# A four-stage transformer block on one core: another order of the steps in the opening and the first feed-forward

## The reference

```python
x = x + tanh(gx[0]) * wkv(time_decay, time_first, k=layernorm(x), v=ctx)      # time mix: a scan over tokens
x = x + tanh(gf[0]) * (mlp(layernorm(x)) + peer(layernorm(x)))                # feed-forward 1024 wide, and look-up experts
x = x + tanh(gx[1]) * gated_linear_attention(layernorm(x), ctx)               # 16 heads, keys and values from ctx
x = x + tanh(gf[1]) * (top-2 of 8 experts + shared expert)(layernorm(x))

# peer: queries -> two sets of 64 scores -> top 8 of each -> top 8 of the 64 sums -> 8 of 512 rows,
#       silu(x . down_row) * softmax(score), times up_row, summed
# attention: kv_summary = sum over tokens of feature(k) (x) v,  feature(k) = k + 1 if k > 0 else exp(k)
```

## Time and profile before

| | |
|---|---|
| runs | 507.08, 507.49, 510.03 us |
| the profiled execution | 508.22 us, span 506.4 us |
| TensorE busy | 450.3 us, 89% |
| its weight loads | 356.1 us, 70% |
| VectorE | 347.2 us, 69% |
| ScalarE | 247.2 us, 49% |
| GpSimd | 173.8 us, 34% |

### The profile page before, as it was taken

The page is one execution under the profiler, slowest core; times in us unless marked ns, Lnnn a source line. Parts: engine busy times, 40 slices in busy tenths (PEclk is TensorE's granted clock), DMA queues, the critical chain, the costliest instruction groups (busy, mean ns, idle before and its releaser), DMA issues. The chain is left out here.

```text
span 506.4 us, 7287 instructions
## 1 busy us (share of the span) xinstructions
PE 450.3 (89%) x2162; PEld 356.1 (70%) x2162; DVE 347.2 (69%) x994; ACT 247.2 (49%) x479; POOL 173.8 (34%) x181
## 2 busy tenths in 40 slices
PE   2769799589989999999999998998998899899991
PEld 1447588458668776888778786887776688788860
DVE  6968569988486964577978967888778354621173
ACT  2868264223577377455044416360751544955540
POOL 3787232354022333400000000060525015477771
PEclk9999799789999999999999999999999899999997
DMA  8421212002000000980000000142323223346494
GB/s 306 164 80 57 62 33 80 5 20 83 1 1 2 0 1 0 293 218 0 1 2 1 0 2 0 32 136 74 119 71 112 88 79 111 105 150 191 123 380 138
DMA packets 32966, 42.02 MB, mean 83 GB/s; under 512 B 3483, under 2 KB 26781, under 8 KB 32928
## 3 DMA queue, kind: packets, MB, share of 16 engines
q1 hardware_dynamic: 28224, 32.28, 21.0%
q0 software_dynamic: 3744, 8.42, 4.5%
q10 hardware_dynamic: 960, 0.86, 0.5%
HBM read 24.97 MB, written 18.39 MB: 86 GB/s over the span
## 5 line engine op out<-in xcount | busy, mean ns | idle before, releaser
L678 PE MATMUL acc<-w_down,act_s 128*128 128x256 f32 x384 | 91.5, 384 | 0.9 <-DVE act_s L1410 0.9
L678 PEld LDWEIGHTS acc<-w_down,act_s 128*128 128x128 f32 x384 | 73.6, 193 | 12.8 <-DVE act_s L1410 1.3
L654 PE MATMUL ring<-xt_h,up_l 128*128 128x512 f32 x160 | 71.1, 444 | 1.4 <-DVE kv_sum L1490 1.4
L1137 ACT ACTIVATE act_s<-ring 128x512 f32<-128x512 f32 x48 | 28.6, 596 | 73.5 <-PE ring L656 73.3
L655 PE MATMUL ring<-xt_l,up_h 128*128 128x512 f32 x160 | 63.4, 396 | 0.0
L656 PE MATMUL ring<-xt_h,up_h 128*128 128x512 f32 x160 | 63.3, 395 | 0.0
L1625 POOL TENSOR_TENSOR rstd<-var_eps,minus_half 128x4 f32<-128x4 f32 x14 | 14.5, 1039 | 135.7 <-DVE var_eps L1225 135.7
L717 PE MATMUL ring<-up_e,act_s 128*128 x184 | 45.7, 392 | 2.3 <-issue 2.0
L1677 POOL DMA_INDIRECT x_rows<-main_a,slots x32 | 31.1, 972 | 43.7 <-ACT main_a L1158 34.8
L1414 DVE TENSOR_TENSOR act_s<-ring,act_s 128x512 f32<-128x512 f32 x32 | 21.9, 686 | 34.3 <-ACT act_s L1137 16.4
L717 PEld LDWEIGHTS ring<-up_e,act_s 128*128 128x128 f32 x184 | 34.2, 196 | 7.2 <-issue 3.2
(11 more groups left out here) (281 smaller groups left out, 1009.6 us busy)
## 6 DMA issues: line engine op xcount, KB each, us to landing
main_b<-x_rows SPq DMA_DIRECT2D x22, 257.0 KB, 3.0
x_rows<-v_t SPq DMA_DIRECT2D x1, 3983.5 KB, 16.1
up_l<-y_rows SPq DMA_DIRECT2D x5, 512.0 KB, 5.9
stage<-in_w_mlp SPq DMA_DIRECT2D x8, 256.0 KB, 2.6
up_e<-in_w_moe SPq DMA_DIRECT2D x8, 256.0 KB, 2.6
x_rows<-v_t SPq DMA_DIRECT2D x1, 1927.5 KB, 22.4
x_nat<-in_x SPq DMA_DIRECT2D x7, 256.0 KB, 7.9
out_x<-x_nat SPq DMA_DIRECT2D x6, 256.0 KB, 5.0
```

Source lines behind the costliest of these rows:

```text
L654: pe.matmul(out, wl, xh, start=first, stop=False, skip_group_check=True)
L678: last = pe.matmul(acc[t // 2][:, t % 2, :], act_s[n % RING][:, tok], w_down[:, u, :], start=u == 0 and t % 2 == 0, stop=final, skip_group ...
L1137: act.activation(act_s[n % RING][:, :], bank[:, :], ACT.Silu).then_inc(free_sem((step, "A", u)), 1)
```

## The change

It edits START, the PLAN of the first two feed-forwards, DEN_SCALE and NORM_ACT.

- Opening: group 0's last time mix product (`wkv_out 0 5`) goes ahead of both weighings of group 1 (`wkv_in 1 3 4`, which were in two places). The first scans of group 1 (`wkv_out 1 0`) go from ahead of `wkv_out 0 6 7` to behind `x_stats 0 0`.
- First feed-forward: key product (1,3) goes from part 10 to part 3, its sum from part 11 to part 4. The second pair of scans of group 2 (`wkv_out 2 1`) goes from part 7 to part 8, behind `peer_in 0 0`. The later steps of `wkv_out 2` are shared out anew over the parts 9 and 10. The key products and sums of (2,0) and (2,1) come from the second feed-forward into parts 8 to 10.
- Second feed-forward: only (2,2) and (2,3) of group 2 are left, in parts 2 to 4.
- The denominators of group 2 get their own term from ScalarE and GpSimd instead of VectorE, and group 2 is normalised by ScalarE instead of VectorE (which brings a negated mean on VectorE and a shift on GpSimd, both of 4 columns).

```diff
--- before.py
+++ after.py
@@ -126,9 +126,9 @@
 
 
 START = """wkv_in 0 0, setup 0 0, wkv_in 0 1, wkv_in 1 0, wkv_in 0 2, kv_k 0 0, kv_e 0 0, wkv_out 0 0, wkv_in 1 1, kv_k 0 1,
-    wkv_out 0 1, wkv_in 1 2, wkv_out 0 2, kv_e 0 1, kv_v 0 0, kv_c 0 0, wkv_out 0 3 4, kv_k 0 2, kv_e 0 2, wkv_in 1 3,
-    wkv_out 0 5, kv_v 0 1, kv_c 0 1, wkv_in 1 4, split 0 0, kv_k 0 3, kv_e 0 3, kv_v 0 2, kv_c 0 2, wkv_out 1 0,
-    wkv_out 0 6 7, kv_k 1 0, kv_e 1 0, kv_v 0 3, kv_c 0 3, x_stats 0 0, split 0 1, wkv_out 1 1, kv_k 1 1, kv_e 1 1, kv_v 1 0,
+    wkv_out 0 1, wkv_in 1 2, wkv_out 0 2, kv_e 0 1, kv_v 0 0, kv_c 0 0, wkv_out 0 3 4, kv_k 0 2, kv_e 0 2,
+    wkv_out 0 5, kv_v 0 1, kv_c 0 1, wkv_in 1 3 4, split 0 0, kv_k 0 3, kv_e 0 3, kv_v 0 2, kv_c 0 2,
+    wkv_out 0 6 7, kv_k 1 0, kv_e 1 0, kv_v 0 3, kv_c 0 3, x_stats 0 0, wkv_out 1 0, split 0 1, wkv_out 1 1, kv_k 1 1, kv_e 1 1, kv_v 1 0,
     kv_c 1 0, mlp_in 0 0 1, mlp_in 0 2, kv_v 1 1, kv_k 1 2, wq 0 0, wkv_out 1 2, kv_c 1 1, kv_e 1 2, wkv_out 1 3 4"""
 
 
@@ -136,24 +136,23 @@
     ("mlp", 0): {
         1: "wkv_out 1 5, casts 0 0, query 0 0",
         2: "wkv_out 1 6 7, x_stats 1 0, kv_v 1 2, kv_c 1 2, query 0 1",
-        3: "route_in 2 1, route_in 2 2, query 2 0, wkv_in 2 0",
-        4: "query 2 1, wkv_in 2 1, route 0 2 3, wkv_in 2 2 3 4",
+        3: "kv_k 1 3, route_in 2 1, route_in 2 2, kv_e 1 3, query 2 0, wkv_in 2 0",
+        4: "query 2 1, wkv_in 2 1, route 0 2 3, wkv_in 2 2 3 4, kv_v 1 3, kv_c 1 3",
         5: "route 0 4 5 6",
         6: "route 0 7 8, wkv_out 2 0",
-        7: "wkv_out 2 1",
-        8: "peer_in 0 0, wkv_out 2 2 3",
-        9: "wkv_out 2 4 5",
-        10: "wkv_out 2 6 7, x_stats 2 0, kv_k 1 3, kv_e 1 3",
-        11: "mlp_in 1 0, kv_v 1 3, kv_c 1 3, kv_m 0 0 1 2 3",
+        8: "peer_in 0 0, wkv_out 2 1, kv_k 2 0 1",
+        9: "wkv_out 2 2 3 4, kv_e 2 0 1",
+        10: "wkv_out 2 5 6 7, x_stats 2 0, kv_v 2 0 1, kv_c 2 0 1",
+        11: "mlp_in 1 0, kv_m 0 0 1 2 3",
         12: "mlp_in 1 1, route 1 2, kv_m 1 0 1 2 3",
         13: "mlp 0 14 15, mlp_in 1 2, route 1 3",
     },
     ("mlp", 1): {
-        1: "mlp_out 0 0, route 1 4, kv_k 2 0, kv_e 2 0",
-        2: "route 1 5, kv_k 2 1, kv_v 2 0, kv_c 2 0, kv_e 2 1",
-        3: "route 1 6, wkv_in 3 0, kv_k 2 2, kv_v 2 1, kv_c 2 1, kv_e 2 2",
-        4: "route 1 7, wkv_in 3 1, kv_k 2 3, kv_v 2 2, kv_c 2 2, kv_e 2 3",
-        5: "wkv_in 3 2 3 4, route 1 8, kv_v 2 3, kv_c 2 3",
+        1: "mlp_out 0 0, route 1 4",
+        2: "route 1 5, kv_k 2 2, kv_e 2 2",
+        3: "route 1 6, wkv_in 3 0, kv_k 2 3, kv_v 2 2, kv_c 2 2, kv_e 2 3",
+        4: "route 1 7, wkv_in 3 1, kv_v 2 3, kv_c 2 3",
+        5: "wkv_in 3 2 3 4, route 1 8",
         6: "wkv_out 3 0 1",
         7: "wkv_out 3 2 3",
         8: "peer_in 1 0, wkv_out 3 4 5, query 1 0",
@@ -220,9 +219,9 @@
 
 OPEN_GROUPS = (0, 1)
 
-DEN_SCALE = {(0, 0): 0, (0, 1): 1, (1, 0): 0, (1, 1): 2}
-
-NORM_ACT = {("wkv_in", 1), ("mlp_in", 0)}
+DEN_SCALE = {(0, 0): 0, (0, 1): 1, (1, 0): 0, (1, 1): 2, (2, 0): 1, (2, 1): 2}
+
+NORM_ACT = {("wkv_in", 1), ("wkv_in", 2), ("mlp_in", 0)}
 
 XN_ORDER = {s[:2]: n for n, s in enumerate(s for s in SCHED if APPLY.get(s[0]) == s[2])}
```

## The result

| | before | changed |
|---|---|---|
| median, us (19 runs each) | 509.81 | 512.21 |
| lowest to highest | 505.56 to 513.47 | 509.50 to 515.12 |
| profiled execution, span | 508.22, 506.4 | 512.21, 510.1 |

The ratio is 1.0058, interval 1.0031 to 1.0085: slower, but by less than the one per cent that counted as a difference. The forecast was 508.1 in a range of 501.5 to 513.0.

The account below looks back on a forecast made before the run. TensorE was taken as the bound, with only holes and slow stretches before 160 us winnable. Terms 3.0 - 3.0 + 3.8 - 0.5 - 0.6 - 2.1 = +0.6 on 507.49 gave 508.1 us, range 501.5 to 513.0.

Parts of the forecast that it names:

- likeliest case: Whole kernel: a change within one per cent, 5.1 us, either way; chance 53%.
- opening: Before the first feed-forward's transposes: hole grows from 2.69 to 5.2 us, half clock behind it; +3.0 us.
- part 3: First feed-forward: key product (1,3) fills the 2.27 us hole and full clock follows; -3.0 us.
- part 4: First feed-forward: ScalarE normalises group 2 late, TensorE idles 2.95 us, key sum (1,3) adds 0.9; +3.8 us.
- tables to time mix transposes: Table transposes to group 2's: the `exps_t_l` hole goes, a nearly 7 us wait for GpSimd's product replaces 2.15; -0.5 us.
- from there to the second feed-forward: After group 2's time mix transposes: 2.6 us of work leaves, 1.0 enters, 1.0 of half clock added; -0.6 us.
- second feed-forward: 4.4 us of key work already done, but much becomes a wait of some 3.5 us for GpSimd's addition; -2.1 us.
- behind it: From the second feed-forward's end on: nothing is moved, so the sum reaches the kernel's end; 0 us.
- the key products fill holes for nothing: Rival, 26%: clock stays up through the opening's hole, ScalarE and GpSimd keep up in the second feed-forward; -6.2 us, 501.3.
- the clock falls behind ScalarE's late normalisation: Rival, 22%: half clock behind the 2.95 us hole at group 2's transposes and the 3.5 us wait; +5.1 us, 512.6.
- key product (1,3) doesn't hold the clock: Rival, 15%: in part 3 of the first feed-forward the clock falls anyway; +3.0 us, 511.1.
- the change does what it says: Its opposite was a rival, under 5%: VectorE so late that `exps_t_l` is still waited for; about 1 us lower, 507.

Follow-up runs that it names:

- idle matmuls: Matmuls with unread results: five before the feed-forward's first transposes in the changed kernel, ratio 1.0018; four in the opening of the fastest kernel, ratio 0.9779.
- the kernel with the opening alone: The kernel before with the new START and nothing else of the change: 509.38 us against 508.93, ratio 1.0011.
- both experiments on START: New START alone in the kernel before, ratio 1.0011 to before; old START in the changed kernel, ratio 1.0037 to before.
- the low part ahead: The kernel before with only the second scans of group 2 moved behind `peer_in 0 0`: 508.31 us against 510.22, ratio 0.9984.
- the early statistics: The changed kernel with group 3's statistics in part 1 and normalisation in part 3 of the second feed-forward: 506.84 us, ratio 0.9951 to before.
- all key products in the holes: Changed kernel with old START, VectorE normalising group 2, and all group 2 key products in the first feed-forward: 507.41 us, ratio 0.9946 to before.

## Why the prediction held, and where it was off

The time, 512.21, fell in the range, and the change within one per cent, as the likeliest case had it. But the forecast of 508.1 is 4.1 us low. Of these 2.3 are the base: the first three runs of the kernel before had a median of 507.49, all nineteen 509.81. The other 1.8 are the sum, +0.6 us where the medians moved by 2.4. The two profiled executions, both at a mean clock of 0.974, differ by 3.99 (their spans by 3.7, to which the steps add up). Step by step, the same places in the two traces:

| step | forecast | measured |
|---|---|---|
| opening | +3.0 | +3.0, and 0.6 ahead of it |
| part 3 | -3.0 | -2.87 |
| part 4 | +3.8 | +3.84 |
| tables to time mix transposes | -0.5 | +0.54 |
| from there to the second feed-forward | -0.6 | -2.02 |
| second feed-forward | -2.1 | -0.33 |
| behind it | 0 | +0.95 |

A table of two executions mixes the order with where the clock happened to halve. The same stretches in the other profiles, in us:

| stretch (profiles with idle matmuls left out of the first row) | order of before | order of the change |
|---|---|---|
| start to route rows' transposes | 56.9 in before's profile; 58.2 to 60.4 in six others with the old START | 60.5 in the changed kernel's; 58.8 to 59.6 in four others with the new START |
| from there to the table transposes | 30.9; 28.0 in two others | 31.9; 33.3 to 33.5 in four others |
| to the time mix transposes | 19.6; 19.6 in the kernel with the opening alone | 20.2; 20.1 to 20.2 in six others |
| to the second feed-forward | 19.2; 19.1 in the kernel with the opening alone | 17.2; 17.5 to 18.6 in six others |
| to the third's key sum | 75.6; 75.6 in three others | 75.3; 75.1, 73.8 and 73.7 in three others |
| to the end, the same steps in all | 304.1 | 305.1; 303.1 to 306.7 in the twelve experiments |

**Opening.** The hole was 4.92 us (forecast 5.2), ScalarE's normalisation began at 36.24 (35.85; the forecast's own addends give 35.97), and the clock read 0.50 behind it. That the +3.0 came out is luck of the pair: before's profile is the only one of seven with a hole of 2.63 to 2.69 us there that kept full clock behind it. With the old START six other executions came to the route rows as late as those with the new one (first row of the second table), and both experiments on START moved the median by 0.1 to 0.2 per cent, 0.6 to 1.1 us. The 0.6 ahead of it wasn't in the sum: the key product at 23.23 already began at 23.84, behind statistics of group 1 on VectorE at 9.81 instead of 9.06, which had waited for the input's transfer. That is before anything that the change moves; I count it to the execution. The forecast looked at the larger of two holes only: the one ahead of group 0's time mix transposes shrank from 2.28 to 0.41 us.

**Part 3 and part 4** came as worked out, wait by wait: 0.56 for "some 0.6", full clock, and 2.70 for 2.95. (In the page's slices the hole of part 3 and its half clock are the fifth digit, 7 and 7; the list of weak slices ahead leaves it out.) ScalarE's table load at 73.17 again took 1.28 us with its first activation 1.29 after, so the drain that the Trainium skill, "ScalarE: Activation LUTs", section "What ACT_TABLE_LOAD costs", adds to a switch doesn't show here either. But the term of part 3 holds only for this pair of executions: before lost 3 us of clock at that hole in its profile, and the experiments with the opening alone and with the low part ahead kept full clock behind the same hole. They need 28.0 us for the two parts, the changed kernel 31.9, and 33.3 to 33.5 where the clock falls behind the 2.70 us. So against a kernel before at full clock the two parts cost 3.8 us or more, not the +0.8 that the forecast's terms give.

**Tables to time mix transposes: the chain was right and 1.0 us too short.** GpSimd's product was forecast 19.1 us behind the table transposes; the transposes that wait for it came 20.2 behind. `exps_t_l` came 0.5 later than reckoned (3.1 for 2.6), and VectorE waited 0.93 us at 99.37 for ScalarE's `host_s`. ScalarE in turn had waited 3.35 us for the look-up unit's up product (96.23), which TensorE ran behind the two key products that the change brought there. TensorE's hole was 5.05 instead of nearly 7, since the two bank waits (1.37 and 0.82, which I had not foreseen) had taken 2.2 us of it ahead: they cost nothing, because VectorE's chain was the longer one: with two more key products in that hole the stage took the same 20.2 us.

**From there on: -2.02, beyond the bound of -1.7.** I added 1.0 us for a longer half clock behind the larger hole. The loss was 1.4 us (0.59 over 3.5), and before it was 1.5. That explains 1.1 of the 1.4 us between forecast and trace. But it is a lucky execution: with the same hole six other profiles need 0.3 to 1.4 us more for this stretch, that is -1.8 to -0.7 against before, so -2.02 is not the order's own. The added 1.0 is what the slowest of them had.

**Second feed-forward: the term that failed in this pair.** I wrote that "the rest of the 4.4 us turns into a wait of some 3.5 us". The wait is there, 3.44 us, at the place and with the releaser named. But I set the price at the wait alone and left the half clock behind it to a rival, although the sum charges it behind the opening's hole and the one ahead of the time mix transposes. It cost 0.34 x 5.0 = 1.7 us, the whole gap between -2.1 and -0.33. The experiment with the early statistics shows both halves: taking the wait away gave 3.6 us and then 1.6 more. Whether the clock falls there is again open: behind the wait of 3.44 us it fell in two profiles (75.3 and 75.1 us for the stretch) and held in two (73.8 and 73.7, which is -1.9 against before's 75.6). The forecast's -2.1 is right for the second kind only.

**The last term.** 0.95 us comes behind 262 us, where the order is the same in both kernels. The fourteen profiles need 303.1 to 306.7 us from the third feed-forward's key sum to the end, so it lies within what executions differ by; what differs in them wasn't looked for.

**Rivals.** That the key products fill holes for nothing is out: the opening's hole lost its clock. That the clock falls behind ScalarE's late normalisation didn't happen in the profile, but did in four of five profiled executions with the hole of 2.70 us, the changed kernel's own being the fifth. So the term of 3.8 for part 4 was the lucky value of two; the other is 1.5 us more. That this rival's time, 512.6, is the nearest to the measured median is luck: it rests on the base of 507.49, and its +5.1 is further from the measured +2.4 than the forecast's +0.6. That key product (1,3) doesn't hold the clock is out: 1.00 in part 3 in every profile that had it there. The low part was not waited for, so the change does what it says.

**Where the expected gain went.** The change removed 5.44 us of hole, 1.7 of another (2.27 to 0.56), 1.9 of a third (2.28 to 0.41, in the opening), and behind the first two some 6.7 us that half clock cost in before's profile (half of the 6.9 and 6.5 us of the earlier trace rows). It created 2.2 in the opening, 2.7 in part 4, 2.9 ahead of the time mix transposes, 2.2 of bank waits, 1.9 in the second feed-forward, and new half clock behind two of them. The sums of idle time from 20 to 210 us are 20.4 before and 24.3 after (190 less 169.57 and 165.71 busy); of clock, 8.5 and 6.8 us were lost. The work did not get less; it was late in other places. Of the holes that it created, only the wait of 3.44 us is shown over the runs to be worth more than their noise (the early statistics); the one of part 4 is priced by traces. Key products (2,0) and (2,1) and the shared denominators of group 2 were never run alone, so their own price is open.

## What to carry to other kernels

Filling a hole with ready work pays only if what was behind the hole isn't late anyway: ask of each engine what it must still do before the next wait, and count a hole that reopens at its length plus the half clock behind it. Before work is moved ahead, look at what the moved sum's releaser is queued behind; here one step of statistics and its normalisation, moved earlier, were worth 5 us (1.1 per cent), more than key product (1,3) brought alone (0.4) or all key products in the holes (0.5). Where the spread of the runs is a few holes' clock, take the price of a hole's clock from several profiles and not from one, and compare kernels over many runs.

## What the runs showed of the hardware

**The spread of the runs goes with TensorE's clock.** Over the 104 runs of the kernel before that stand beside the experiments, the time goes with the mean granted clock: 513.45 us on average at 0.962 (7 runs), 509.52 at 0.971 (16), 508.45 at 0.974 (11), 505.55 at 0.981 (5). Six runs of the changed kernel at 0.974 lie between 511.24 and 512.36, so at the same clock the change costs 3.5 us. Its nineteen runs had more clock on average (0.9751 against 0.9707 in those 104), which may be why the medians are only 2.4 apart.

**The same hole halves the clock in one execution and not in another.** Behind 2.69 us in the opening: 1.00 in the kernel before, 0.57 to 0.66 over 4 us behind 2.63 to 2.69 us in six others. Behind 2.27 us: 0.51 before, 1.00 in two others. Behind 2.70 us: 1.00 in the changed kernel, 0.59 to 0.66 in four others. Behind 3.44 us: 0.66 and 0.72 in two, 1.00 in two. Behind every hole of 4.9 to 5.7 us in the profiles the clock was down. One such stretch cost 1.4 us (0.59 over 3.5 us, changed kernel) to 3.4 us (0.51 over 6.9, kernel before). The Trainium skill, "TensorE: Matmul & The Clock Gate", says under "What's actually happening", of the matmuls at a kernel's start, that the time spent at the low clock varies from run to run of one kernel, and puts the penalty of such a ramp under one per cent of a typical span. One stretch here, 1.4 to 3.4 us of 506, is under one per cent too; but several of them in one kernel, each of which comes in some runs only, leave the runs 1.6 per cent apart.

**Matmuls that do nothing kept the clock**: with four of them at two holes of 2.3 and 2.6 us the mean clock of the runs rose from 0.983 to 0.988 and their median fell by 2.8 us (six runs each, whose times don't overlap).

**VectorE's scans and GpSimd's additions took longer beside each other.** In the kernel before two scans took 2.36 us at 87.69 with GpSimd idle, and the next two 3.40 us at 90.67 beside a GpSimd addition at 90.89 of 2.09 us; the same kind of addition took 1.27 and 1.29 us in the opening (21.09, 23.68), with no scan beside it. In the changed kernel the pair at 96.06, moved away from that addition, took 2.38. So 1.0 of the 3.40 us was not the scans' own.
